# Attention's matmuls as four side by side of 32 columns, on one Trainium2 core

## What is computed

```python
q, k, v = proj(Wq, bq), proj(Wk, bk), proj(Wv, bv)          # 16 heads of 16
attn_scores = einsum('bhqd,bhkd->bhqk', q, k) / sqrt(16)
decay_mask = einsum('hnqk,hn->hqk', dp ** abs(t[:, None] - t[None, :]), softmax(mix_weights))
attn_probs = softmax(attn_scores * decay_mask[None], axis=-1)
out = einsum('bhqk,bhkd->bhqd', attn_probs, v)
x = x + out.reshape(B, S, 256) @ Wo.T + bo
x = x + relu(layernorm(x) @ ternary(W1).T + b1) @ ternary(W2).T + b2
```

## Time and profile before

| | |
|---|---|
| median of 3 executions | 1788.83 us (1787.71 to 1789.39) |
| profiled execution | 1787.85 us, of which the span of the profile is 1786.1 us |
| instructions in the profile | 31816 |
| PE busy | 1749.3 us in 11794 matmuls |
| PE weight loads | 780.4 us, beside the matmuls |
| DVE, ACT, POOL busy | 1550.4, 1341.3, 771.4 us |
| DMA | 230.32 MB, mean 129 GB/s |

### The profile page before, as it was taken

How to read it: one execution, slowest core, us unless ns; L and a number is a source line. 1 busy time by engine, 2 the same in 40 slices (tenths; PEclk the granted TensorE clock), 3 DMA queues, 4 the chain that set the end, 5 groups by cost and what they waited for, 6 DMA issues and landing times.

```text
span 1786.1 us, 31816 instructions
## 1 busy us (share of the span) xinstructions
PE 1749.3 (98%) x11794; PEld 780.4 (44%) x11794; DVE 1550.4 (87%) x3657; ACT 1341.3 (75%) x1552; POOL 771.4 (43%) x401
## 2 busy tenths in 40 slices
PE   7979999999999999999999999999999999999998
PEld 4524444444444444444444444444444444445666
DVE  5879989999899998899899999988998999887885
ACT  5748687878787777878787868687878787667565
POOL 4009182726354453637281909182727364130110
PEclk9959999999999999999999999999999999999999
DMA  6884747474655546464737373747474644444441
GB/s 197 276 211 104 159 97 162 97 156 100 133 121 120 133 103 141 102 153 102 151 86 159 81 155 89 153 98 162 97 161 98 135 115 107 108 135 110 136 120 36
DMA packets 177834, 230.32 MB, mean 129 GB/s; under 512 B 92640, under 2 KB 113520, under 8 KB 167536
## 3 DMA queue, kind: packets, MB, share of 16 engines
q1 hardware_dynamic: 175744, 227.61, 54.7%
q0 software_dynamic: 80, 0.54, 0.2%
q10 hardware_dynamic: 1856, 0.14, 0.1%
HBM read 65.94 MB, written 36.45 MB: 57 GB/s over the span
## 4 chain that ended last, share of the span: by engine, by line
PE 89%; DVE 4%; ACT 1%; issue 0%; ACTq 0%; DVEq 0%
PE ring L1514 28%; PE ring L1467 27%; PE tile L1498 23%; PE tile L1495 3%; PE tile L1554 3%; PE ring L1573 2%; DVE part_max L1257 1%; PE ring L1532 1%; PE ring L1481 1%; DVE z_lo L1335 1%; ACT z_hi L1179 0%; ACT probs L1219 0%; DVE qk L1339 0%; PE ring L1540 0%; DVE part_max L1259 0%
## 5 line engine op out<-in xcount | busy, mean ns | idle before, releaser
L1219 ACT ACTIVATE probs<-tile 128x1024 f32<-128x1024 f32 x1024 | 1000.5, 1023 | 328.0 <-PE tile L1495 180.6
L1257 DVE TENSOR_REDUCE part_max<-ring 128x1 f32<-128x512 f32 x1536 | 965.7, 684 | 121.4 <-PE ring L1467 119.4
L1467 PE MATMUL ring<-k_stack,q_stack 96*128 96x512 f16 (+2 forms) x3072 | 714.5, 314 | 11.3 <-SPq L211 9.7
L1498 PE MATMUL tile<-q_stack,k_stack 98*128 98x512 f16 (+2 forms) x2560 | 584.4, 326 | 0.3
L1514 PE MATMUL ring<-probs,v_ones 128*32 128x512 f32 x4096 | 546.1, 605 | 0.0
L1467 PEld LDWEIGHTS ring<-k_stack,q_stack 96*128 96x128 f16 x3072 | 263.8, 99 | 511.7 <-DVE part_max L1257 393.4
L1098 POOL TENSOR_TENSOR diag<-diag,row_max 128x1024 f32<-128x1024 f32 x64 | 121.3, 1895 | 628.5 <-DVE row_max L1270 628.5
L1498 PEld LDWEIGHTS tile<-q_stack,k_stack 98*128 98x128 f16 x2560 | 249.4, 98 | 275.1 <-ACT probs L1219 6.2
L188 POOL TENSOR_TENSOR decayed<-qk,table_in 128x1024 f32<-128x1024 f32 x120 | 282.5, 2360 | 8.0
L1259 DVE TENSOR_REDUCE part_max<-ring 128x1 f32<-128x384 f32 x512 | 280.7, 548 | 0.8 <-PE ring L1467 0.7
L202 POOL TENSOR_TENSOR lo<-decayed,hi 128x1024 f16<-128x1024 f32 x120 | 256.0, 2134 | 10.3 <-ACT hi L196 10.3
(11 more groups left out here) (147 smaller groups left out, 935.8 us busy)
## 6 DMA issues: line engine op xcount, KB each, us to landing
q_stack<-hi SPq DMA_DIRECT2D x320, 128.0 KB, 3.8
k_stack<-hi SPq DMA_DIRECT2D x128, 256.0 KB, 4.4
q_stack<-lo SPq DMA_DIRECT2D x160, 128.0 KB, 3.1
table_in<-table_scratch SPq DMA_DIRECT2D x64, 256.0 KB, 8.3
k_stack<-lo SPq DMA_DIRECT2D x64, 256.0 KB, 3.7
out_scratch<-heads_out SPq DMA_DIRECT2D x64, 256.0 KB, 3.3
k_stack<-hi SPq DMA_DIRECT2D x64, 128.0 KB, 3.8
lo<-out_scratch SPq DMA_DIRECT2D x32, 256.0 KB, 5.2
```

What stands on the lines that cost most here:

```text
L1219: nc.scalar.activation(probs[:, t % 4], tile[t % 2][:].rearrange("p a b -> p (a b)"), ACT.Exp, scale=1.0 / (SCALE * SCALE * HEAD_DIM ** 0. ...
L1257: nc.vector.tensor_reduce(out[:, k:k + 1], ring_bank(n), AX.X, ALU.max).then_inc(ring_free, 1)
L1467: last = nc.tensor.matmul(ring[:, n % RING, col:col + width], q_stack[h][0:STACK, q // UNIT_SLOTS, level, q0:q0 + P], k_stack[h][0:STACK, ...
L1498: last = nc.tensor.matmul(out, k_stack[h][:, level, kb * P:(kb + 1) * P], q_stack[h][:, half, level, col:col + width], start=bank not in s ...
```

## The change

Three kinds of matmuls are each split into four (two for turns) calls with 32 stationary columns, which write 32 PSUM partitions each. The moving side is the same for all calls of a group. The f32 transposes of diagonal blocks and turns become f32 products with the identity, without the transpose flag. The number of semaphore increments and waits is the same.

```diff
+QUARTER = 32
...
                     for j, (level, first, width) in enumerate(banks[k]):
-                        last = nc.tensor.matmul(ring[:, n % RING, col:col + width],
-                                                q_stack[h][0:STACK, q // UNIT_SLOTS, level, q0:q0 + P],
-                                                k_stack[h][0:STACK, level, first:first + width],
-                                                start=(j == 0), stop=True, skip_group_check=True)
+                        for r in range(0, P, QUARTER):
+                            last = nc.tensor.matmul(ring[r:r + QUARTER, n % RING, col:col + width],
+                                                    q_stack[h][0:STACK, q // UNIT_SLOTS, level, q0 + r:q0 + r + QUARTER],
+                                                    k_stack[h][0:STACK, level, first:first + width],
+                                                    start=(j == 0), stop=True, skip_group_check=True)
...
-                nc.tensor.transpose(ring[0:MAXROWS * LO_ROWS, n % RING, 0:P],
-                                    max_repeated[:].rearrange("p r b -> p (r b)"), ident[:]).then_inc(ring_full, 1)
+                for r in range(0, MAXROWS * LO_ROWS, QUARTER):
+                    last = nc.tensor.matmul(ring[r:r + QUARTER, n % RING, 0:P],
+                                            max_repeated[:].rearrange("p r b -> p (r b)")[:, r:r + QUARTER], ident[:],
+                                            start=True, stop=True, skip_group_check=True)
+                last.then_inc(ring_full, 1)
...
-                    if level == RAW:
-                        last = nc.tensor.matmul(out, diag[h][:, kb], ident[:], is_transpose=True,
-                                                start=bank not in started, stop=True, skip_group_check=True)
-                    else:
-                        last = nc.tensor.matmul(out, k_stack[h][:, level, kb * P:(kb + 1) * P],
-                                                q_stack[h][:, half, level, col:col + width],
-                                                start=bank not in started, stop=True, skip_group_check=True)
+                    for r in range(0, P, QUARTER):
+                        if level == RAW:
+                            last = nc.tensor.matmul(out[r:r + QUARTER], diag[h][:, kb, r:r + QUARTER], ident[:],
+                                                    start=bank not in started, stop=True, skip_group_check=True)
+                        else:
+                            last = nc.tensor.matmul(out[r:r + QUARTER],
+                                                    k_stack[h][:, level, kb * P + r:kb * P + r + QUARTER],
+                                                    q_stack[h][:, half, level, col:col + width],
+                                                    start=bank not in started, stop=True, skip_group_check=True)
                     started.add(bank)
```

## The result

The changed kernel takes 1794.9 us (median of 13 executions, 1789.74 to 1797.13) against 1789.39 us for the kernel before (13 executions, 1787.54 to 1793.22): a ratio of 1.0022, 95% interval 1.0014 to 1.0029. The forecast was 1731. The kernel became no faster; it is slower by about what a measurement of it can tell.

What follows compares the result with a forecast made beforehand. The prediction took TensorE, 98% busy, as the bound. 250 x 0.24 + 250 x 0.03 minus 5 for turns gave 62.5 us, plus 1 for the last slots, minus 6 for VectorE: 1788.8 - 57.5, about 1731 us, range 1714 to 1790.

Steps and rivals of the forecast that it cites:

- The passages between widths: TensorE's switches between 32 and 128 columns in each slot go: 0.24 us saved, net 0.03 in slots with two diagonal blocks.
- Four products side by side cost what a full-width one does: On TensorE, four 32-column f16 products take the 0.216 us of one full-width matmul, with no weight load exposed.
- Rival A: Weight loads are exposed in each f16 group on TensorE, 0.02 us each, 130 us in all: 1861 us; chance 0.09.
- Diagonal block +0.105: A diagonal block's f32 products on TensorE take 0.215 us instead of 0.11, so 0.105 more.
- Turn +0.08: A turn's two f32 groups on TensorE take 0.215 us instead of 0.13, so 0.08 more, 63 times.
- Instructions costed at nothing: TensorE's 96 or 144 instructions a slot, matmuls and weight loads, are hidden under the streaming columns: no cost.
- rival B: PE's instruction packets arrive too late and stall TensorE; break-even at 5.6 us a refill, about 2300 at 8.3; chance 0.05.
- No wait is added and none moved.: PE's waits stay on the first matmul of each tile or item, one increment on the last; no cost entered.
- VectorE as the next to be late: VectorE's reductions nearly become the bound: 0.1 us per 8 slots, 6 us in all, between 0 and 25.
- rival D: VectorE can't follow below 2.84 us in slots without diagonals: 1785 us, half way 1758; chance 0.10.
- Rival C: TensorE's sequencer can't pass a matmul every 0.054 or 0.041 us; near 3600 us at 0.109 each; chance 0.04.
- Rival E: The passages belong to f32 parts, not width, so diagonal blocks and turns get their own: 1954 us; chance 0.02.

Runs made afterwards that it cites:

- e5: The changed kernel with score tiles put back to full-width f16 matmuls and f32 transposes, max pass, turns and products left at 32 columns: 1890.29 us.
- e1: The changed kernel with SP's loads for the pair after the next spread over slots instead of one burst: 1758.29 us, 0.9814 of the kernel before.
- e6: e1 with ScalarE's cast of slot 9 moved to slot 10: 1747.97 us, 0.976 of the kernel before.
- e7: e6 with ScalarE's copy of the maxima (repeat_max) ahead of its slot's first exponential: 1744.89 us, 0.9749 of the kernel before.
- e8: The kernel before with all three edits (spread loads, cast in slot 10, early copy): 1790.72 us, ratio 1.0003.
- e10: e7 with the loads of a step's second half again in one burst, released at slot 25: 1818.62 us, 1.0166 of the kernel before.
- e2: The changed kernel with three of ScalarE's casts moved to other slots, loads still in a burst: 1823.65 us, 1.0188 of the kernel before.

## Why the prediction was wrong

Point by point, in the prediction's order.

- **The passages between widths, 0.24 a slot without diagonals and 0.03 with.** Right. Slots went from 2.842 to 2.602 and from 2.973 to 2.943. In e5 a pair of passages measured 0.215; the rest of the 0.24 are the small terms beside it. Their sum, 67 us, is there in the slots.
- **Four products side by side cost what a full-width one does.** Right: 0.22 a group, no exposed loads. Rival A (1861) is refuted.
- **Diagonal block +0.105.** Right: 0.065 before (0.131 for two), (2.943 - 2.602) / 2 = 0.17 after. **Turn +0.08**: 0.16 before on average, 0.21 in e5, so +0.05.
- **Instructions costed at nothing.** This is the step that failed first. The prediction found the queue, its packets and 5.2 us for each, and judged the refill by its mean: "it is hidden under the columns that stream", and in rival B a break-even of 5.6 us over all 141 packets. Half of the refills start within 1 us of their place; the one or two a step that fall into SP's burst start mostly 5 to 7.9 us after it. The price is of the burst, not of the mean: 2.2 us x 15 = 33 us, by e1 37. The rows at hand showed enough for it: table_in lands after 8.3 us, so a packet queued beside it could too, and a packet was to last 5.2. I multiplied 8.3 by all packets, got 2300, found it absurd and gave the mechanism 0.05, where the right reading was "in the burst alone".
- **"No wait is added and none moved."** True of the code, false of the time. A wait that is met 0.2 us early at one pace is missed at another. ScalarE was costed by its share, "75% now, some 78% then", and POOL not at all. The place of a cast between exponentials is a due time tuned to a slot of 2.84 us; eight slots at 2.60 brought it forward by up to 1.9 us against POOL's unchanged chain. Slots 9 and 4 lose 1.15 and 0.58 a step more than before, 26 us in 15 steps. Moving one cast and the turn brought back 13 of them (e6, e7). Of the other 13, 9 are lost again to POOL's chain (0.6 us a step), in slots 6 and 11 by casts that wait for it and in slot 18 by the stack that is loaded behind it; no run tried to make that chain shorter.
- **VectorE as the next to be late** (0.1 us per 8 slots; rival D). Rival D is not borne out: VectorE's idle before the reductions fell from 121 to 95 us, not to little, and the excess of most slots is 0. The 6 us of the forecast are about there, but in the turns: slots 4, 5, 20 and 21 of e7 lose 0.81 us a step, two turns alone cost 0.42 in e5, and 0.39 in 16 steps are 6 us. VectorE works without a pause there, while PE waits for its reductions. That this is its whole cause is not shown.
- **Rival C, the pace of issue.** Refuted where instructions are there: 72 matmuls and 72 weight loads pass in 2.94 us, 0.041 per matmul, with no slot longer than the columns make it. The Trainium skill's 62 ns a matmul ("TensorE: Matmul & The Clock Gate", "Wait — 56ns, not 53.3ns?"), weighed in the prediction as 2190 us, does not hold for this program. Rival E (1954): refuted by the 0.17 of a diagonal block.

So the forecast's mechanism was right and the sum wrong by two unpriced terms. e7 has both mostly removed and stands at 1744.9, 14 us above 1731: its excess is 1.86 us a step, 1.23 more than before, 20 us in 16 steps, where the forecast had 5 for turns and 6 for coupling; the 9 above it are mostly POOL's chain in slots 18, 6 and 11. The other 5 lie outside the 15 steps that the tables average, and were not traced. That gain and loss nearly cancelled (69 against 73 us) is a chance of their sizes: e1 to e7 take the loss away and leave the gain, and e8 shows that the same edits find nothing to take away without the change.

## What to carry to other kernels

When a change multiplies instructions, work out how long one 16 KB packet of them lasts in the densest stretch, and set it against how late a packet can come in the largest burst of transfers, not against the mean. And when the busiest engine gets faster, list every queue where work of a slower chain stands at a place fixed by hand between urgent instructions: a share of 43% or 75% says nothing about whether such a place is still in time. A change that moves nothing may be hiding its whole gain: look for excess per slot before dropping it.

## What was not expected of the hardware

- PE's instruction packet waits behind data on the same 16 DMA engines: with 3.9 MB issued in 14 us (100.9% share) it started 7.1 us after its place, the next one 7.7. PE then stood for up to 2.2 us, and for up to 3.9 in e10. PE goes on only 1.3 to 1.6 us after the packet's end.
- After some of PE's longer waits the granted clock was 0.50 (1.2 GHz) for 3.4 us: in e10 from 988.80 on, after the wait of 2.73 us that ended at 987.67, in e2 from 438.10 on, after the one of 2.40 that ended at 436.58. Not after all: the changed kernel's stop of 2.6 us between two starts (396.50 to 399.07) was followed by none.
- With instructions at hand, PE took 144 of them in 2.94 us at a granted clock of 1.00, with the four matmuls of a group starting within 8 to 13 ns of each other.
- Under a steady stream, 32-column f16 products four side by side keep the pace of a full-width one to 0.002 us (0.215 to 0.218 a group).
